# Block-quantised feed-forward kernel: the last multiply of every quantisation moved from GpSimd to VectorE, and the scale search run once per pair of weight tiles

## What is computed

```python
def _quantize_mx(x, ebits, mfrac, emax_elem, max_norm):
    xb = x.reshape(shp[:-1] + (shp[-1] // 32, 32))
    amax = jnp.max(jnp.abs(xb), axis=-1, keepdims=True)
    sexp = jnp.floor(jnp.log2(amax)) - emax_elem
    scale = jnp.exp2(sexp)
    q = _quantize_elem(xb / scale, ebits, mfrac, max_norm) * scale
    return q.reshape(shp)

gate = _mx_linear(x, w_gate)        # x: 8192 x 2048 tokens, w_gate, w_up: 8192 x 2048
up = _mx_linear(x, w_up)
inter = jax.nn.silu(gate) * up
return _mx_linear(inter, w_down)    # w_down: 2048 x 8192
x = _layernorm(x + attn(x)); x = _layernorm(x + ffn(x))
```

## Time and profile before

| | us |
|---|---|
| median of 2 runs | 7996.74 (7996.26 to 7997.22) |
| profiled execution, its time | 7998.23 |
| profiled execution, span of the slowest core | 7996.7 |
| spans of the 8 cores | 7976.8 to 7996.7 |
| DVE busy, POOL busy, PE busy | 6043.6, 4253.1, 1627.3 |

### The profile page before, as it was taken

One profiled execution on the slowest core, in us unless ns is written; L12 is line 12 of the kernel. 1 busy time (PEld: TensorE's weight loads), 2 busy tenths in 40 slices (PEclk: granted clock), 3 DMA queues, 4 the chain that ended last, 5 costly groups with the idle time before them and its releaser, 6 DMA issues.

```text
span 7996.7 us, 40881 instructions; the slowest of 8 cores (7976.8 to 7996.7 us)
## 1 busy us (share of the span) xinstructions
PE 1627.3 (20%) x6816; PEld 713.2 (9%) x6816; DVE 6043.6 (76%) x8030; ACT 590.8 (7%) x634; POOL 4253.1 (53%) x2015
## 2 busy tenths in 40 slices
PE   4400302104040402104040402104040402204041
PEld 2100101001010101001010101001010100001010
DVE  3386687786869787786869787786868787786867
ACT  0010000000000000000000000000000000000001
POOL 0036565564646465564646465564646465564643
PEclk7555656557575756657575756557575755657575
DMA  3001121111212121111212121111212121111211
GB/s 106 0 8 53 27 61 37 47 50 35 61 28 57 27 59 38 48 50 35 61 25 60 27 59 38 47 51 35 57 28 61 27 59 38 46 50 34 57 29 63
DMA packets 670392, 355.23 MB, mean 44 GB/s; under 512 B 499121, under 2 KB 630578, under 8 KB 668978
## 3 DMA queue, kind: packets, MB, share of 16 engines
q10 hardware_dynamic: 169984, 201.35, 8.0%
q1 hardware_dynamic: 496818, 134.49, 7.6%
q0 software_dynamic: 3328, 16.78, 0.6%
HBM read 222.50 MB, written 8.39 MB: 29 GB/s over the span
## 4 chain that ended last, share of the span: by engine, by line
DVE 59%; issue 17%; PE 10%; POOL 7%; DMA 3%; ACT 2%; DVEq 2%; ACTq 0%; POOLq 0%; SPq 0%
DVE s_c L130 14%; DVE scw L122 11%; DVE fmd L127 7%; PE psY L148 7%; DVE PSC L139 6%; DVE fmd L130 4%; DVE fy L122 4%; DVE INTER L127 3%; DVEq L92 2%; ACT fmd L144 2%; DVE sci L122 2%; POOL fy L122 2%; DVE fy L127 1%; POOL WST L122 1%; POOL INTER L122 1%
## 5 line engine op out<-in xcount | busy, mean ns | idle before, releaser
L148 PE MATMUL psY<-WDT,INTQF 128*128 128x512 bf16 x2048 | 516.6, 420 | 5470.7 <-DVE BIG L122 2961.0
L122 POOL TENSOR_TENSOR fy<-fy,fmd 128x1024 f32<-128x1024 f32 x392 | 1008.4, 2572 | 701.6 <-DVE fmd L130 664.5
L122 POOL TENSOR_TENSOR INTER<-INTER,fmd 128x1024 f32<-128x1024 f32 x336 | 877.9, 2613 | 580.4 <-DVE fmd L130 551.9
L122 DVE TENSOR_TENSOR scw<-scw,s_c 128x64 f32<-128x64 f32 x960 | 836.4, 871 | 102.9 <-DVE s_c L130 3.9
L130 DVE SCALAR_TENSOR_TENSOR s_c<-s_c,scw 128x64 f32<-128x64 f32 x960 | 725.6, 756 | 105.9 <-DVE s_c L130 7.0
L130 DVE SCALAR_TENSOR_TENSOR fmd<-INTER,smalls,fmd 128x1024 f32<-128x1024 f32 x384 | 768.5, 2001 | 45.1 <-DVE fmd L127 1.9
L148 PEld LDWEIGHTS psY<-WDT,INTQF 128*128 128x128 bf16 x2048 | 214.8, 106 | 5772.6 <-issue 5578.3
L127 DVE TENSOR_SCALAR fmd<-fmd,smalls 128x1024 f32<-128x1024 f32 x448 | 625.7, 1397 | 49.1 <-DVE INTER L127 0.9
L139 DVE TENSOR_REDUCE PSC<-WST 128x64 f32<-128x2048 f32 x192 | 437.4, 2278 | 170.4 <-DMA WST<-wd 147.4
L144 ACT ACTIVATE fmd<-fy 128x1024 f32<-128x1024 f32 x252 | 263.2, 1054 | 3733.7 <-DVE fy L127 1546.6
L148 PE MATMUL psG<-WGT,XQF 128*128 128x512 bf16 x1024 | 407.3, 398 | 417.8 <-DMA WGT<-WQN 402.1
(11 more groups left out here) (170 smaller groups left out, 3987.1 us busy)
## 6 DMA issues: line engine op xcount, KB each, us to landing
WST<-wg ACTq DMA_DIRECT2D x128, 512.0 KB, 4.6
WST<-wu ACTq DMA_DIRECT2D x128, 512.0 KB, 4.4
WST<-wd ACTq DMA_DIRECT2D x128, 512.0 KB, 5.0
xps<-xP POOLq DMA_DIRECT2D x8, 1024.0 KB, 7.3
BIG<-xT SPq DMA_DIRECT2D x16, 512.0 KB, 19.1
y<-BIG POOLq DMA_DIRECT2D x8, 1024.0 KB, 4.2
WGT<-WQN SPq DMA_TRANSPOSE x128, 2.8
WUT<-WQN SPq DMA_TRANSPOSE x128, 2.8
```

The lines of the kernel that those rows point to most:

```text
L122: return self.emit(eng, lambda h: h.tensor_tensor(out, a, b, op), reads, writes)
L148: return self.emit("pe", lambda h: h.matmul(out, lhsT, rhs, start=start, stop=stop), reads, writes, quiet=quiet)
```

## The change

Two edits. (1) In `emit_quant` the final multiply is always emitted for DVE, where before it went to the quantisation's own engine. Add and subtract stay on the own engine. (2) The scale search of weight tiles leaves `wq_load_tile` (where it stood behind each tile's maximum, 64 columns wide) and goes to the head of `wq_back`, where one search of 128 columns covers both tiles of the job. `scw` and `invw` hold two buffers of 128 columns instead of three of 64.

```diff
                 p.tt(_yv, _yv, _mdv, Alu.subtract, _kys + [_kmd], _kys, eng=_se)
-                p.tt(r3(_out), r3(_yv), _scb, Alu.mult, _kys + _sk, _ok, eng=_se)
+                p.tt(r3(_out), r3(_yv), _scb, Alu.mult, _kys + _sk, _ok, eng="dve")
...
-            scw = sf("scw", [128, 192])
-            invw = sf("invw", [128, 192])
+            scw = sf("scw", [128, 256])
+            invw = sf("invw", [128, 256])
...
                 p.red(am_w[:, slot * 64:(slot + 1) * 64].unsqueeze(2), r3(wst), Alu.max,
                       [f"wst{slot}a", f"wst{slot}b"], [f"amw{slot}"], absval=True)
-                emit_search(am_w[:, slot * 64:(slot + 1) * 64], [f"amw{slot}"],
-                            scw[:, sl3 * 64:(sl3 + 1) * 64], f"scw{sl3}",
-                            invw[:, sl3 * 64:(sl3 + 1) * 64], f"invw{sl3}",
-                            None, "wt2", s_c2[:, 0:64], "wc2", None)
...
             def wq_back(job, nxt):
                 dram, s, t0, kind, wkey = job
+                wpar = wpc[0] % 2
+                wpc[0] += 1
+                scwS = scw[:, wpar * 128:(wpar + 1) * 128]
+                invwS = invw[:, wpar * 128:(wpar + 1) * 128]
+                skeys = [f"scw{wpar}", f"invw{wpar}"]
+                emit_search(am_w[:], ["amw0", "amw1"], scwS, skeys[0], invwS, skeys[1],
+                            None, "wt2", s_c2[:], "wc2", None)
...
-                        c0 = hh * 32
+                        c0 = slot * 64 + hh * 32
```

More of the change, by code:

```diff
@@ L520, in build_program @@
             WQN = sf("WQN", [128, H // 2], BF16)
-            scw = sf("scw", [128, 192])
-            invw = sf("invw", [128, 192])
+            scw = sf("scw", [128, 256])
+            invw = sf("invw", [128, 256])
             s_c2 = sf("s_c2", [128, 128])
+            wpc = [0]
             igc = [0]
-            wtc = [0]
-            TSL = {}
             PSC = pf("PSC", [128, 160])
@@ L548, in wq_load_tile @@
                 slot = ti % 2
-                sl3 = wtc[0] % 3
-                wtc[0] += 1
-                TSL[(kind, s, ti)] = sl3
                 wst = WST[:, slot * H:(slot + 1) * H]
```

## The result

The changed kernel takes 8062.7 us (median of 7 runs), against 7995.7 (median of 6 runs, the two of the table above among them) for the kernel before. Ratios here are of the means of the runs: 1.0087, 95% interval 1.0075 to 1.0099. That is 0.87% slower, inside 2%. An eighth run, of 8091.0 us, is not among the seven. The forecast was 8104 us and 1.3%. The profiled run's slowest core is core 5, with a span of 8059.0 us; spans of other cores differ by up to 0.2%, so stages can be compared with those of core 7 before.

The account below looks back on a forecast made before the run. Orders and handovers between DVE and POOL, not one engine's sum, were taken to set the time. −118 − 6 − 4 + 112 + 132 − 5 − 4 = +107 on 7998.2, stated as 8104 us; own range 8050 to 8160.

Parts of the forecast that it names:

- What bounds the kernel: Whole kernel: no engine is full (DVE 76%, POOL 53%, PE 20%); orders and handovers between DVE and POOL set the time.
- The ring: Weight jobs: each POOL quantisation waits for a DVE final multiply that waits for POOL; one turn takes 11.5 us.
- Rival 1: Slower: the parts of a POOL quantisation's turn run in series, 12.4 us; 8320 us, 4% slower; chance 0.10.
- The final multiply at 1.23: Final multiply on DVE: 1.23 us if POOL is really idle there, 3.12 if not; 1.23 taken.
- The search: Head of each weight job: the 128-column scale search takes 8.05 us; POOL idles 10.1 us per job with the second maximum.
- Jobs: Weight jobs of two tiles: all on POOL 56.1 us, DVE's quantisation first 49.9; a pair 107.6 against 109.7 before.
- rival 3: Weight sections gain nothing, as the shorter job with DVE's quantisation first is unproven: 8232 us, 2.9% slower; chance 0.13.
- Sections: Whole weight sections: first kind 318.7 us (was 326.1), second kind 321.3 (was 329.6); mean gain 7.9.
- the term of −118: Sum over 15 whole weight sections, at a mean gain of 7.9 us each.
- Down and inner parts: DVE waits: 7.5 us ahead of each of 15 down parts (+112), 3.3 more per inner group, 40 times (+132).
- Rival 4: Final multiplies ahead of down parts and inner groups hide behind PE: 7865 us, 1.6% faster; chance 0.03.
- Rival 2: Faster: the port shared by DVE and POOL is the bound; jobs save 4.2 us each: 7834, 2.0% faster; chance 0.07.

Follow-up runs that it names:

- e9: The kernel before, with the scale search of weight tiles on a scratch in PSUM and its maxima in SBUF: 7374.2 us, ratio 0.9217.
- e5: The changed kernel with a third work buffer for POOL's quantisations, in place of one of DVE's two fmd buffers: 7759.2 us, ratio 0.9698.
- e3: The changed kernel, but final multiplies emitted by flushq (ahead of down parts, in inner parts) are on their own engine: 7859.3 us, ratio 0.9828.
- e12: e5 with the weight scales searched and kept in PSUM and the maxima moved to SBUF: 7559.0 us, ratio 0.9458.

## Why the prediction was right, point by point

- **What bounds the kernel.** Right: 831 us less DVE work and 855 less POOL work came out 0.9% slower, so no engine's sum set the time. That the search is slow because of POOL was the reading of one column of the groups; e9 confirms it with an exchange of memories alone. One thing the reading by operands leaves out: the first of the three steps has one SBUF operand and waits for POOL too (1.65 us for 0.69). The sum held all the same, as its steps were taken from rows beside POOL.
- **The ring.** Forecast 11.5 us, measured 11.55. It could be read from the trace before because POOL had the same instructions beside the same steps there. e5 shows that the buffer makes it. Rival 1 (12.4 in series) is out.
- **The final multiply at 1.23.** 1.22 in the rings; 1.65 as a mean over the `fy` ones, as those of DVE's own quantisations still stand beside POOL at about 3.1.
- **The search.** 8.05 forecast from the line through 32 and 64 columns. In the rows after, from the maximum's end (2438.55) to POOL's multiply (2446.66), it takes 8.1.
- **Jobs.** POOL-first followed by a DVE-first one: 57.7 forecast, 57.6 measured. DVE-first: 49.9, measured 49.4. First job of a section: 51.8 and 48.3, measured 51.4 and 48.5. So rival 3 fell: the chain with the most steps held.
- **Sections.** The second kind 321.3, measured 321.0 (mean 321.0 over all of them). The first kind 318.7, measured 315.2: this is the step that failed. Its last job ends with a DVE-first job, which I took as 38.6 with "a maximum to 23.9" in it. The last job of a section loads no next tile, so it has no such maximum. It takes 36.2, and its last two final multiplies indeed come 2 us earlier than elsewhere. In eight sections of the first kind that is some 19 of the 36 us by which the term of −118 was off. The rest are the half-microseconds of the DVE-first jobs and a value before that I took from one section (326.1 and 329.6), where the means are 326.5 and 330.1.
- **Down and inner parts.** 7.5 and 3.3 us forecast, 7.1 (7.2 with the 0.1 before) and 3.1 to 3.2 measured. The inner group's terms as I listed them add to 22.6 and not to 22.4, which would have made the forecast some 8 us worse. e3 takes both waits away and gives 204 us back, as expected (213). Rival 4 (hidden behind PE) is out.
- **Rival 2, the port as the bound.** Wrong for the changed kernel, in which the port is idle during a job's head, but of the right kind for the next bound: it is what e5 ran into at 10.4 us a turn. As a sum it is too dear there: 7.8 + 2.75 + 1.23 = 11.8 for such a turn. The rule that the Trainium skill gives on its page "SBUF — State Buffer", section "Who interferes with whom", explains who waits. These runs agree with it for DVE (0.22 us alone, 1.1 to 2.4 beside POOL, in a 64-column instruction), but POOL loses less than the whole duration of DVE's instructions: 2.4 us in that turn, for instructions that take 3.9 alone. Which order stands in the queues decides whether any of it costs time.

The sign came out right because every term was a difference of rows, and because one gain and two losses of over 100 us each were booked singly: each of them alone is larger than the result. The size is less sure than it looks. The forecast of +107 was 40 us above the +67 measured, nearly all of it in the one term named above, and 8063 lies only 13 us above the lower end of my own range.

## What to carry to other kernels

A step moved to another engine adds a wait to every buffer that it reads: follow the buffer to its next writer before counting the busy time that moved, and look at what stands in line ahead of the moved step, and behind it at every place where a pipeline is flushed. When two engines disturb each other, an operand in PSUM can end that for less work than a reordering: in e9 it gave 626 us, with nothing reordered. Two edits that touch the same queue are to be measured singly and together: here +281 and −65 made +67.

## What was not expected of the hardware

- The exchange of one operand's memory in the search's 64-column instructions is worth 626 us of 8001 (e9): beside POOL such an instruction took up to 2.4 us, and 0.22 alone.
- POOL loses less than DVE's instructions last. In e12 against e5 the final multiply, 1.2 us alone, cost POOL 0.84 us. In e5's turn the three steps and that multiply take 3.9 us alone, and POOL's turn is 2.4 longer than its own 8.0. In which part of a DVE instruction POOL can go on, no run shows.
- One SBUF operand is not always enough to be left alone. The first of the three steps (line 127, `INTER<-fmd`) has one and took 1.65 us beside POOL for 0.69 alone. The block maximum (line 139) has one too, and none of the 192 took more than 2.30 us in either kernel, beside POOL or not.
- Waiting is counted as busy, on both engines. In e5's turn of 10.37 us DVE is busy for 10.15 and POOL for 9.99. The same DVE work takes 6.2 alone (steps 2.7, multiply 1.2, block maximum 2.3), the same POOL work 7.8. Busy time in such a stage is no measure of work.
